# Layer one of a graph network: two partial sums for the scalar columns are joined by TensorE inside the node sums instead of by VectorE

## The reference

```
radial = silu(edge_attr @ w1 + b1) @ w2 + b2            # per edge, 4 paths of 16 x 16 weights
out0 = alpha * (einsum('eu,e,euw->ew', x0, sh0, w00)
                + einsum('eui,ei,euw->ew', x1, sh1, w11) / SQRT3)
out1 = alpha * (einsum('eu,ei,euw->ewi', x0, sh1, w01)
                + einsum('eui,e,euw->ewi', x1, sh0, w10)) / SQRT3
msgs = concatenate([out0, out1.reshape(-1, 48)], axis=1)
agg = segment_sum(msgs, dst, num_segments=N)
```

## Time and profile before

| | us |
|---|---|
| median of 3 runs | 19270.44 (19254.84 to 19276.73) |
| profiled execution, its own time | 19271.95 |
| span of the profiled execution | 19270.1 |
| VectorE busy in the span | 14747.2 (77%) |
| GpSimd busy | 12260.2 (64%) |
| TensorE matmul busy | 9310.3 (48%) |
| ScalarE busy | 3949.6 (20%) |

### The profile page before, as it was taken

How to read it: one execution, slowest core, us unless ns; L and a number is a source line. 1 busy time by engine, 2 the same in 40 slices (tenths; PEclk the granted TensorE clock), 3 DMA queues, 4 the chain that set the end, 5 groups by cost and what they waited for, 6 DMA issues and landing times. The chain is left out here.

```text
span 19270.1 us, 218526 instructions
## 1 busy us (share of the span) xinstructions
PE 9310.3 (48%) x50893; PEld 6358.9 (33%) x50894; DVE 14747.2 (77%) x25325; ACT 3949.6 (20%) x9903; POOL 12260.2 (64%) x12680
## 2 busy tenths in 40 slices
PE   0343325566666666655777763333243334344343
PEld 0333322232233233222333353333243334334333
DVE  8556668999999999998888832221488888688887
ACT  0111101111111111111000000000144444344443
POOL 0677876666666666663777727777376665566663
PEclk9999996666666666666888855555555655565555
DMA  5333221111111111112222211112532223233223
GB/s 212 76 83 72 69 71 29 25 27 26 25 27 26 25 26 27 25 25 24 29 30 29 28 13 26 26 26 26 66 75 70 73 74 62 69 75 75 68 73 55
DMA packets 1107684, 958.58 MB, mean 50 GB/s; under 512 B 758507, under 2 KB 874859, under 8 KB 1097292
## 3 DMA queue, kind: packets, MB, share of 16 engines
q0 software_dynamic: 368704, 436.55, 12.9%
q1 hardware_dynamic: 738316, 514.36, 10.4%
HBM read 736.74 MB, written 212.93 MB: 49 GB/s over the span
## 5 line engine op out<-in xcount | busy, mean ns | idle before, releaser
L1585 POOL DMA_INDIRECT tail<-ball,h_idx x3328 | 3493.3, 1050 | 2040.4 <-issue 1005.9
L835 PE MATMUL p_rad<-w_stack,hid_t 99*128 99x512 bf16 (+1 forms) x6656 | 2659.1, 551 | 2397.0 <-DVEq L932 1331.9
L905 DVE TENSOR_REDUCE red<-prod 128x96 f32<-128x1536 f32 x1664 | 2901.0, 1743 | 3.5
L1616 PE MATMUL h_sum<-head,h_hot 128*128 128x64 f32 x6656 | 1248.5, 375 | 3164.2 <-ACT head L1671 2993.5
L1616 PEld LDWEIGHTS h_sum<-head,h_hot 128*128 128x128 f32 x6656 | 1220.1, 287 | 3177.0 <-issue 3177.0
L343 POOL DMA_INDIRECT rec_a<-rec,slot x1600 | 1825.3, 1141 | 516.5 <-issue 487.2
L1229 POOL DMA_INDIRECT l_xg<-h_tab,l_idx x1664 | 1570.0, 944 | 835.9 <-issue 500.5
L835 PEld LDWEIGHTS p_rad<-w_stack,hid_t 99*128 99x128 bf16 (+1 forms) x6656 | 716.3, 122 | 4024.7 <-issue 3894.3
L1028 POOL DMA_INDIRECT l_xg<-x_tab,l_idx x1664 | 1570.2, 944 | 658.6 <-issue 493.3
L1042 PE MATMUL l_sum<-outer,l_hot 128*128 128x512 f32 x3328 | 1664.5, 665 | 531.2 <-DVEq L1087 531.2
L752 POOL DMA_INDIRECT l_xg<-in_x,l_idx x1664 | 1577.7, 948 | 522.9 <-issue 475.4
(11 more groups left out here) (408 smaller groups left out, 19410.8 us busy)
## 6 DMA issues: line engine op xcount, KB each, us to landing
hot_t<-rows_l SPq DMA_DIRECT2D x208, 512.0 KB
rec_a<-fill SPq DMA_DIRECT2D x128, 728.0 KB, 19.4
l_rec<-rec_a SPq DMA_DIRECT2D x104, 896.0 KB, 4.8
rhot_t<-rows_r SPq DMA_DIRECT2D x208, 384.0 KB
tail<-ball,h_idx POOLq DMA_INDIRECT x3328, 2.5
t<-in_type SPq DMA_DIRECT2D x100, 512.0 KB
l_xg<-in_x,l_idx POOLq DMA_INDIRECT x1664, 2.4
l_xg<-x_tab,l_idx POOLq DMA_INDIRECT x1664
```

The costliest lines, as they stand in the source:

```text
L835: ins = pe.matmul(p_rad[j % 3][:, h * 512:(h + 1) * 512], hid_t[j // 4 % 2][0:K3 + 3 * (1 - i), j % 4, i, :], w_stack[i][0:K3 + 3 * (1 - i ...
L905: ch.step(dve.tensor_reduce(red[q][:, j, :], prod[j % 3][:, :, :], AX, ALU.add))
L1585: pool.indirect_dma_start(tg[q][:, j, :], None, table[:, :], bass.IndirectOffsetOnAxis(ap=idx[q][:, j:j + 1], axis=0)).then_inc(gathered[q ...
L1616: ins = pe.matmul(p_sum[u % 2][:, j % BT // 2, :], hot[j // HP8 % 3][:, j % HP8, :], hg[:, j, 0:D], start=(j % 2 == 0), stop=(j % 2 == 1))
```

## The change

VectorE no longer adds the two scalar terms. TensorE gets a third matmul for each tile in the node sums, with the same stationary `hot` and the 16 columns 0 to 15 of `red`, which go on top of the first 16 columns of the sum. On VectorE a wait for `msg` stands where the add was.

```diff
                 for j in range(BT):
                     pe.matmul(p_sum[:, j // 2, :], hot[q][:, j, :], red[q][:, j, 2 * MUL:6 * MUL], start=(j % 2 == 0), stop=False)
+                    pe.matmul(p_sum[:, j // 2, 0:MUL], hot[q][:, j, :], red[q][:, j, 0:MUL], start=False, stop=False)
                     ins = pe.matmul(p_sum[:, j // 2, MUL:D], hot[q][:, j, :], msg[:, j, :], start=False, stop=(j % 2 == 1))
                 ins.then_inc(sum_done, 1)
@@
                 ch.step(dve.tensor_tensor(m1, bc(red[q][:, :, MUL:2 * MUL].unsqueeze(3), [P, BT, MUL, 3]),
                                           bc(sh1.unsqueeze(2), [P, BT, MUL, 3]), ALU.mult))
-                ch.do(dve.tensor_tensor(red[q][:, :, 2 * MUL:3 * MUL], red[q][:, :, 2 * MUL:3 * MUL], red[q][:, :, 0:MUL], ALU.add))
+                ch.sync()
                 dve.sem_inc(rec_used, 1)
                 dve.sem_inc(msg_done, 1)
```

## The result

The changed kernel takes 20303.92 us (median of 6 runs, 20293.25 to 20315.41), the kernel before 19260.89 us on the same occasions (6 runs): ratio 1.054, 95% interval 1.0526 to 1.0554. It is slower by 1043 us; the forecast was 20195 us, in the range 19600 to 20450.

What follows compares the result with a forecast made beforehand. VectorE sets the stage's pace, but TensorE's chain into tile 3 sets the block boundary. 3.55 + 4.93 + 0.79 - 0.33 = 8.94 us, x 103 = 921 us, plus 6.5 us in the last block, gave 20195 us, range 19600 to 20450.

Steps and rivals of the forecast that it cites:

- TensorE's chain sets the boundary: Between blocks, VectorE's tile 3 waits for TensorE's run from tile 15 through the node sums; slack 0, bounds 0 and 0.2 us.
- 0 for the add: At the 103 block boundaries, removing VectorE's add L941 wins 0, since VectorE merely arrives sooner at a wait.
- 0.34 us on VectorE: From L939 to the next block's first product, VectorE gains 0.34 us a block, 35 us at best over 103.
- reading (a): In the node sums the load sets a pass: 0.1108 us at 16 columns, +3.55 us a block at 2.4 GHz.
- reading (b): In the node sums a 16-column product costs 0.156 us by straight line, +2.5 us a block; chance 0.08.
- The clock falls within the sum: In the longer node sums TensorE's clock drops from 2.4 to 1.2 GHz; chance 0.66 with 0.11 us passes.
- 3.55 + 4.93: Growth of the node sums per boundary: third product at 2.4 GHz, plus the second half stretched by 1.93.
- The fall in the middle: Clock drop placed halfway through a 10.63 us sum, stretching its second half of 5.31 us by 4.93 us.
- forecast 0.79: Tile 3 behind the sums is filled at 1.2 GHz, 1.66 us against 0.87 us: +0.79 us a boundary.
- The earlier start of the sum: From tile 0 to the node sums, 5.27 us in place of 5.60 as the clock's rise shifts: -0.33 us a boundary.
- the first rival: The clock holds at 2.4 GHz through the longer node sums: +372 us, 19645 us, or 19610 us; chance 0.18.

Runs made afterwards that it cites:

- the first cut: Changed kernel, one tile of the next block filled after every 4 tiles of sums, VectorE's adds three tiles later: 19282.07 us, ratio 1.0005 against the kernel before.
- the first experiment: Changed kernel without its third product, VectorE's add also gone: 19266.39 us, ratio 1.0002 against the kernel before.
- the second: Changed kernel, next block's tiles 3, 4, 5 after the first 4 tiles of sums, 6 and 7 after 4 more each, adds from tile 6: 19412.54 us, 1.008.
- the third: Changed kernel, next block's tile 3 ahead of the sums, tiles 4, 5, 6 one after each 4 tiles of sums, adds from tile 6: 19677.2 us, 1.0203.

## Why the prediction was right

**That TensorE's chain sets the boundary**: shown. Without the third product the removed add changes nothing (1.0002), with it the add put back changes nothing that the runs can tell, and the profile has the wait at the product of tile 3 in the first (0.45 us) and at the sums in the second.

**0 for the add, 0.34 us on VectorE**: both right. From L939 or L940 to the next product the time fell by 0.33 to 0.34 us.

**A pass costs 0.11 us at 16 columns too**: reading (a) was right on the time. Three products take 0.670 us a tile at 2.4 GHz with 16 columns in the third as with 64 (six passes of 0.112 us). The straight line through 64 and 48 columns, reading (b), does not hold at 16; the mean over many passes was the right thing to take from the earlier trace rows. That it is the load which sets the 0.11 us fits all rows, but no run left a load out, so it is not shown apart.

**The clock falls within the sum**: right, and shown by the width of the third product alone: 64 columns 19631, 32 columns 20228, 16 columns 20304 us. With the clock held the third product costs 370 us, and the sum is 3.56 us longer (10.54 against 6.98); the fall costs the other 670 us.

**The size.** The span grew by 1027.9 us, 6.5 of it in the last block (its wait for the sums is 21.44 us in place of 14.98), so 9.92 us a boundary where 8.94 were forecast. The sum grew by 16.06 - 6.98 = 9.08 us, where 3.55 + 4.93 = 8.48 were forecast. The fall in the middle was a guess for want of a row, and a lucky one: at 84 boundaries the clock falls 3.1 to 6.5 us after the first pass, 5.2 us in the mean, where 5.31 were assumed. At the other 19 the sum begins at the low clock, which the forecast did not have. Tile 3 costs 1.94 us from its start to VectorE's product against 1.10 in the mean before, +0.84 (forecast 0.79). From the last pass to tile 3's start are 0.21 us in place of 0.11, +0.10, which no term covered. The earlier start of the sum, booked at -0.33 us, was the term furthest off for its size: from tile 0 to the sum are 5.40 us in the mean against 5.50, -0.10 us. 9.08 + 0.84 + 0.10 - 0.10 = 9.92 us, the whole of it.

**The rule of the clock page.** The Trainium skill's page TensorE: Matmul & The Clock Gate (Part 1: The HAM clock gate) has sustained activity release the throttle and idleness restore it. Read as "no pause, no throttle" it would have given the first rival. In this kernel the clock falls and stays low while TensorE has no gap at all: some 14 us in the shown sum (5230 to 5243.9 us), and 16 us in the four windows of the first cut. That it is occupied is not enough here. For the section LDWEIGHTS (107 ns for 128 columns) the traces agree at 2.4 GHz, 0.112 us a pass; at 1.2 GHz a pass takes 0.213 us. The floor for a small matmul in the section Back-to-back issue gap is for a matmul by itself, as that section says, and is not what a pass with its own load costs here.

## What to carry to other kernels

The f32 products here cost the same time a pass at 16, 32, 48 and 64 columns, each pass with its own stationary load, so work that is moved to TensorE as such products has to be priced in passes, not in columns: here 0.42 us on VectorE was exchanged for 32 passes, 3.6 us. Before an engine is relieved at the place where it looks busy, find the event that the next wait really hangs on: if that event's chain begins ahead of the work that goes, the gain is nothing, as in the first experiment. And a long stretch of narrow matmuls can lose TensorE's clock with the engine fully occupied, and a pass then costs 0.21 us in place of 0.11; look at the granted clock of the stretch, in the present kernel and in the nearest row with thinner work.

## What was not expected of the hardware

A wider moving operand, its added columns of no use, made the changed kernel faster: 64 columns in place of 16, same number of passes, 19631 against 20304 us.

The order of dense and thin work matters more than its sum. The first cut gave back 1020 us; the second and third, with the same matmuls in other places, 890 and 630. In the third, with three products, the clock was low over the sums at 55 of 103 boundaries and at 1.00 at the other 48, with a pause of TensorE ahead of the sums at all of them. In the first cut five boundaries of 103 stayed at 1.2 GHz, one through a stretch of 32 us without a gap in TensorE's work, tiles of 512 columns among it. What decides which boundaries these are was not settled.
